# Spread indirect transfers, second norms as row scales, one ranking for all tokens, and a chunk's rows weighed on VectorE

## The reference

```python
# layer 0: state-space branch, two sequences of 1024, chunks of Q=128, 64 heads of 8
Yd     = einsum('bcijh,bcjhp->bcihp', CB * Lmat * dtc, xs_c)       # within a chunk
wdec   = exp(cum[:, :, -1:, :] - cum) * dtc
states = einsum('bcqh,bcqhn,bcqhp->bchpn', wdec, Bc, xs_c)         # rows weighed by decay
yn     = yz * rsqrt(mean(yz * yz) + EPS) * norm_w
# layer 0 and layer 3: mixture of 8 experts, 2 of them per token (plus a shared one in layer 0)
top_w, top_ids = top_k(probs, 2);  out = sum over the 2 experts of w * expert(x)
# layer 2: xn2 = ln(xn) * ln_scale + ln_bias, prev = shift(xn2)
kx = xn2 * mix_k + prev * (1 - mix_k)      # the same with mix_v and mix_r
# then a scan over 256 steps with a running maximum, and a quantised gated ffn
# layer 3: x1 = ln(xn, ln1_g, ln1_b); xln = ln(x1, tm_g, tm_b); then a shift, a mix, products
```

## Time and profile before

| | |
|---|---|
| median of 3 runs | 1617.82 us (1613.74 to 1619.62) |
| the profiled execution | 1622.43 us, span 1620.6 us |
| mean granted clock of PE | 0.895 |
| layer 0 | about 0 to 639 us |
| layer 1 | to about 918 us |
| layer 2 | to about 1169 us |
| layer 3 | to the end |

### The profile page before, as it was taken

One profiled execution on the slowest core, in us unless ns is written; L12 is line 12 of the kernel. 1 busy time (PEld: TensorE's weight loads), 2 busy tenths in 40 slices (PEclk: granted clock), 3 DMA queues, 4 the chain that ended last, 5 costly groups with the idle time before them and its releaser, 6 DMA issues. The chain is left out here.

```text
span 1620.6 us, 21650 instructions
## 1 busy us (share of the span) xinstructions
PE 1323.1 (82%) x7251; PEld 818.1 (50%) x7251; DVE 936.6 (58%) x1888; ACT 534.5 (33%) x885; POOL 412.4 (25%) x380
## 2 busy tenths in 40 slices
PE   5765988897898556999999897898556599988997
PEld 3433645555564334657666544454343364644464
DVE  6767565664646874213103489898676445567434
ACT  1454356536535530222222231333112123233311
POOL 3278224313528641200400110000015300000035
PEclk9877999998989676999999898999856698999999
DMA  9232113212213222100000230000001100111113
GB/s 357 67 90 80 43 35 107 63 40 79 83 29 107 75 66 74 39 0 1 0 0 0 105 129 1 0 1 1 1 3 65 59 20 27 33 39 56 53 49 117
DMA packets 72082, 88.86 MB, mean 55 GB/s; under 512 B 19174, under 2 KB 55334, under 8 KB 71337
## 3 DMA queue, kind: packets, MB, share of 16 engines
q1 hardware_dynamic: 65836, 70.78, 14.1%
q0 software_dynamic: 6144, 16.79, 3.3%
HBM read 61.14 MB, written 26.38 MB: 54 GB/s over the span
## 5 line engine op out<-in xcount | busy, mean ns | idle before, releaser
L398 PE MATMUL l_banks<-l_xnT,all_region_a 128*128 128x512 f32 x288 | 129.0, 601 | 0.0
L1877 PE MATMUL l_banks<-l_xnT,mid_region_c 128*128 128x512 f32 (+1 forms) x192 | 96.3, 654 | 17.5 <-DVE l_xnT L2060 17.5
L2720 POOL TENSOR_TENSOR l_rstd<-l_moments,all_neg_half 128x4 f32<-128x4 f32 x20 | 20.6, 1030 | 337.5 <-DVE l_moments L2760 337.4
L914 POOL TENSOR_TENSOR all_region_b<-all_region_b,l_lc 128x512 f32<-128x512 f32 x64 | 87.8, 1393 | 36.5 <-DMA all_region_b<-l_lc_rows 36.1
L928 POOL TENSOR_TENSOR l_rw<-l_xdt,l_decay 128x512 f32<-128x512 f32 x64 | 71.8, 1152 | 63.9 <-DVE l_xdt L1171 63.9
L1191 DVE TENSOR_TENSOR all_region_b<-all_region_b,l_cbd 128x512 f32<-128x512 f32 x64 | 77.6, 1213 | 16.3 <-ACT all_region_b L746 12.2
L398 PEld LDWEIGHTS l_banks<-l_xnT,all_region_a 128*128 128x128 f32 x288 | 54.5, 193 | 61.5 <-issue 60.3
L398 PE MATMUL l_banks<-all_region_b,l_xp 128*32 128x32 f32 x2048 | 32.3, 208 | 62.9 <-DVE all_region_b L1191 62.8
L746 ACT ACTIVATE all_region_b<-all_region_b 128x512 f32<-128x512 f32 x64 | 69.0, 1079 | 14.6 <-PE l_banks L398 10.4
L1877 PEld LDWEIGHTS l_banks<-l_xnT,mid_region_c 128*128 128x128 f32 (+1 forms) x192 | 37.7, 202 | 68.3 <-issue 49.6
L398 PE MATMUL l_banks<-all_region_a,all_xa 128*128 x234 | 68.8, 418 | 1.3 <-DVEq L1040 0.4
(11 more groups left out here) (442 smaller groups left out, 2883.6 us busy)
## 6 DMA issues: line engine op xcount, KB each, us to landing
all_region_b<-l_lc_rows SPq DMA_DIRECT2D x256, 64.0 KB, 2.1
all_xa<-slots_in SPq DMA_DIRECT2D x39, 128.0 KB, 2.1
slots_out<-all_xa SPq DMA_DIRECT2D x39, 128.0 KB, 2.0
mid_vector_rows<-slots_in SPq DMA_DIRECT2D x39, 128.0 KB, 2.1
slots_out<-all_region_a SPq DMA_DIRECT2D x39, 128.0 KB, 1.7
slots_in<-l_xp SPq DMA_DIRECT2D x4, 1024.0 KB, 12.7
all_region_a<-l_gate_up SPq DMA_DIRECT2D x1, 4096.0 KB, 14.4
all_x<-x SPq DMA_DIRECT2D x4, 512.0 KB, 5.6
```

The source lines that it names most:

```text
L398: return nc.tensor.matmul(out, lhsT, rhs, start=start, stop=stop, **kw)
L914: nc.gpsimd.tensor_tensor(bc[:, k, :, :], bc[:, k, :, :], spread(lc[:, c, heads], 1, BLK), ALU.subtract).then_inc(dd_ready.sem, 1)
L1877: return nc.tensor.matmul(out, lhsT, rhs, start=start, stop=stop)
L2720: nc.gpsimd.tensor_tensor(rstd[:, :], moments[:, :, 1], mem.neg_half[:, 0:GT], ALU.pow).then_inc(rstd_ready.sem, 1)
```

## The change

It has eight parts.

A. `steps_at`: the expert tile steps of layer 0 stand after the 32 pieces from (0,3) to (2,2), with every third doubled (10 of them), where they stood after 36 pieces from (0,3) to (2,3), with six doubled. Chunk (0,3) has 5 instead of 4, group 1 has 21 instead of 20, chunks 0 to 2 of group 2 have 16 instead of 14, and chunk (2,3) has none instead of 4.

B. `weigh` is DVE's, behind `take_cb` of the same chunk; `take_xs` needs no wait for the weighed rows any longer.

C. Scatters of layer 0: 8 issues instead of 16 ahead of the first differences, 4 behind them, the rest between the differences of the chunks; the last 6 stand behind `differences(0,3)`.

D. Fetches: 12 issues (t = 2 to 7) move from group 3 into chunk (2,3), and the other 20 all stand ahead of group 3's chunk loop, 8 of them behind `differences(3,0)`.

E. At the end of layer 0 the last `out_stats` stands ahead of `quantise(1)` on DVE.

F. Layer 2: the second norm is one scale per row, worked out on POOL from the first norm's variance, and ACT applies it (`norm_again`, four activations). DVE measures xn no more. The mix is one subtraction of 128x1024 per group and 6 instructions of 128x512.

G. Layer 3: all groups' second norm scale is worked out at once on POOL (128x16), `nl` is four scalings and one addition of 128x1024, ACT copies both turned halves into one of two buffers, and the ranking is done once for all 16 tiles (`rank`).

H. `PLAN` and `beside` are reordered for it: `nl`, `nm` of groups 0 and 1 stand behind `dispatch`.

The diff, cut (the removed `weigh` is POOL's, the added one DVE's; the added `norm_again` is ACT's, in layer 2):

```diff
-    places = [(g, c, k) for g in range(GROUPS - 1) for c in range(NCH) for k in range(PIECES) if (g, c) >= (0, 3)]
-    places = sorted(places + [places[4 * i + 6] for i in range(STEPS - len(places))])
+    places = [(g, c, k) for g in range(GROUPS - 1) for c in range(NCH) for k in range(PIECES)
+              if (0, 3) <= (g, c) < (GROUPS - 2, NCH - 1)]
+    places = sorted(places + [places[3 * i + 2] for i in range(STEPS - len(places))])
...
-        def weigh(g, c):
-            pool.wait_ge(xs_ready.sem, xs_ready.done(g, c))
...
-                last = nc.gpsimd.tensor_tensor(rw[:, i, :].rearrange("p (h e) -> p h e", e=HEAD_P), x3,
-                                               spread(decay[:, i, c, :], 2, HEAD_P), ALU.mult)
...
+            if t == GT // 2:
                 for i in range(2):
                     pool.wait_ge(moe.oe_out[i], 16 * ((MOE_TILES - i + 1) // 2))
...
-        late = {0: ((8, 9), (10, 11)), 1: ((12, 13), (14, 15))}
+        late = {0: ((6,), (7, 8)), 1: ((9, 10), (11, 12)), 2: ((13, 14, 15), ())}
...
             if g == GROUPS - 1:
-                for t in range(2 * GT):
+                for t in (*range(GT // 2), *range(2 * GT, 3 * GT)):
                     fetch(t)
...
+                elif g == GROUPS - 2:
+                    for t in range(GT // 2, 2 * GT):
+                        fetch(t)
...
-                if g == GROUPS - 1:
-                    for t in ((12, 13), (14,), (15,), ())[c]:
-                        fetch(t)
...
+        def weigh(g, c):
...
+            for i in range(4):
+                last = nc.vector.tensor_tensor(by_head(rw[:, i, :]), by_head(xdt[:, :]),
+                                               spread(decay[:, i, c, :], 2, HEAD_P), ALU.mult)
+            last.then_inc(rw_ready.sem, 1)
...
                 if c + 1 < NCH:
                     take_cb(g, c + 1)
+                    weigh(g, c + 1)
...
+        out_stats(GROUPS - 1, NCH - 1)
         quantise(1)
-        out_stats(GROUPS - 1, NCH - 1)
...
+        def norm_again(g):
+            act.wait_ge(xn_ready.sem, xn_ready.done(g))
+            act.wait_ge(rstd2_ready.sem, rstd2_ready.done(g))
+            for t in range(GT):
+                last = nc.scalar.activation(x2[:, t, :], xn[:, t, :], ACT.Copy, scale=rstd2[:, g * GT + t:g * GT + t + 1])
+            last.then_inc(x2_ready.sem, 1)
...
+            nc.gpsimd.tensor_tensor(rstd2[:, tiles], moments[:, tiles, 1], rstd[:, tiles], ALU.mult)
+            pool.drain()
+            nc.gpsimd.tensor_tensor(rstd2[:, tiles], rstd2[:, tiles], rstd[:, tiles], ALU.mult)
+            pool.drain()
+            nc.gpsimd.tensor_scalar(rstd2[:, tiles], rstd2[:, tiles], 1e-5, None, ALU.add)
+            pool.drain()
+            nc.gpsimd.tensor_tensor(rstd2[:, tiles], rstd2[:, tiles], mem.neg_half[:, tiles], ALU.pow).then_inc(
+                rstd2_ready.sem, 1)
...
+            if i == 0:
+                nc.vector.tensor_tensor(step[:, :, :], x2T[:, :, 1:], x2T[:, :, 0:GROUP], ALU.subtract)
...
-    PLAN = [("nx", 0), ("nx", 1), ("consts", 0), ("turn_x", 0), ("nx", 2), ("route", 0), ("turn_x", 1), ("bias", 0),
-            ("nx", 3), ("route", 1), ("turn_x", 2), ("ml", 0), ("nl", 0), ("route", 2), ("turn_x", 3), ("nm", 0),
-            ("route", 3), ("dispatch", 0), ("scatter", 0), ("turn_l", 0), ("ml", 1), ("nl", 1), ("mix", 0),
-            ("scatter", 1), ("nm", 1), ("turn_l", 1), ("scatter", 2), ("scatter", 3), ("weights", 0), ("mix", 1),
+    PLAN = [("mx", 0), ("mx", 1), ("nx", 0), ("turn_x", 0), ("mx", 2), ("nx", 1), ("turn_x", 1), ("route", 0),
+            ("mx", 3), ("consts", 0), ("pl", 0), ("nx", 2), ("turn_x", 2), ("route", 1), ("nx", 3), ("turn_x", 3), ("route", 2),
+            ("route", 3), ("rank", 0), ("dispatch", 0), ("scatter", 0), ("nl", 0), ("bias", 0), ("nm", 0),
+            ("scatter", 1), ("turn_l", 0), ("nl", 1), ("mix", 0), ("scatter", 2), ("nm", 1), ("scatter", 3),
+            ("turn_l", 1), ("weights", 0), ("mix", 1), ("scatter", 4), ("scatter", 5), ("time_row", 0), ("scale", 0),
```

More of the change, by code:

```diff
@@ L970, in _ @@
             if g == GROUPS - 1:
-                for t in range(2 * GT, 3 * GT):
+                for t in range(3 * GT, 4 * GT):
                     fetch(t)
-            weigh(g, 0)
+            if g == 0:
+                for t in range(GT, GT + 2):
+                    scatter(t)
             for c in range(NCH):
@@ L1808, in layer2 @@
     rstd = sb("rstd", [P, TILES])
-    moments2 = sb("moments2", [P, GT, 2])
-    rstd2 = sb("rstd2", [P, GT])
+    above = sb("above", [P, TILES])
+    rstd2 = sb("rstd2", [P, TILES])
     xn = sb("xn", [P, GT, DIM])
@@ L1813, in layer2 @@
     x2T = sb("x2T", [P, DK, 1 + GROUP])
-    keep = sb("keep", [P, 3, DK])
     part = sb("part", [P, DK, GROUP])
     x2 = part[:, :, :].rearrange("p a n -> p (a n)").rearrange("p (t d) -> p t d", t=GT)
-    q = part
+    q = step = part
     mixed = sb("mixed", [P, 3, DK, GROUP])
@@ L1963, in _ @@
                              ACT.Exp).then_inc(decay_exp, 1)
+        norm_again(0)
         for g in range(groups):
@@ L1991, in _ @@
                 nc.scalar.activation(buf[:, :, :], buf[:, :, :], ACT.Exp).then_inc(exp_ready.sem, 1)
+            if g + 1 < groups:
+                norm_again(g + 1)
     @block.gpsimd
@@ L2027, in statistics @@
             tiles = slice(n * GT, (n + 1) * GT)
-            nc.vector.tensor_scalar(moments[:, tiles, 1], moments[:, tiles, 1], 1e-5, None, ALU.add).then_inc(
+            nc.vector.tensor_scalar(above[:, tiles], moments[:, tiles, 1], 1e-5, None, ALU.add).then_inc(
                 moments_ready.sem, 1)
@@ L2187, in _ @@
         take_xnT(0)
-        norm_again(0)
         for g in range(groups):
@@ L2214, in _ @@
             sums(g)
-            if g + 1 < groups:
-                norm_again(g + 1)
             if g == 0:
@@ L2278, in layer3 @@
     rc = sb("rc", [P, GT, DIM])
-    lmax = sb("lmax", [P, GT])
-    pairs = GT * N_EXP * N_EXP
-    gt, eq = [junk[:, i * pairs:(i + 1) * pairs].rearrange("p (t e f) -> p t e f", e=N_EXP, f=N_EXP) for i in range(2)]
+    lmax = sb("lmax", [P, TILES])
+    moments_x = sb("moments_x", [P, TILES, 2])
+    rstd_x = sb("rstd_x", [P, TILES])
+    above = sb("above", [P, TILES])
+    rstd_l = sb("rstd_l", [P, TILES])
+    pairs = TILES * N_EXP * N_EXP
+    gt, eq = [b[:, 0:pairs].rearrange("p (t e f) -> p t e f", e=N_EXP, f=N_EXP)
+              for b in (rc[:, :, :].rearrange("p t d -> p (t d)"), xcT[:, :, :].rearrange("p k n -> p (k n)"))]
+    rows_T = [xnT, mixT]
     vm = sb("vm", [P, HALVES, DK])
@@ L2789, in route @@
+        def norm_x(g):
+            dve.wait_ge(rstd_ready.sem, rstd_ready.done(0, norm_at["nx", g]))
+            for t in range(g * GT, (g + 1) * GT):
+                last = nc.vector.tensor_scalar(xn[:, t, :], x[:, t, :], moments_x[:, t, 0:1], rstd_x[:, t:t + 1],
+                                               ALU.subtract, ALU.mult)
+            last.then_inc(normed_ready.sem, 1)
         def route(g):
-            tiles = slice(g * GT, (g + 1) * GT)
-            l4 = lg[:, tiles, :]
             jobs.wait_filled(dve, 0, ("route", g))
-            last = nc.vector.tensor_tensor(l4, jobs.bank(("route", g))[:, 0:GT * N_EXP].rearrange(
-                "p (t e) -> p t e", e=N_EXP), spread(row("router_bias"), 1, GT), ALU.add)
+            last = nc.vector.tensor_tensor(lg[:, g * GT:(g + 1) * GT, :], jobs.bank(("route", g))[
+                :, 0:GT * N_EXP].rearrange("p (t e) -> p t e", e=N_EXP), spread(row("router_bias"), 1, GT), ALU.add)
```

186 lines of the change are left out of this document (91 added, 95 removed).

## The result

The changed kernel takes 1579.24 us (median of 4, 1578.46 to 1580.08) against 1616.32 us (median of 4, 1613.74 to 1619.62). The ratio is 0.977, with a 95% interval of 0.9749 to 0.979: 2.3% faster. The forecast was 1584 us with a range of 1562 to 1607.

What follows compares the result with a forecast made beforehand. PE was taken to bound the whole, waiting some 300 us. The terms -13 + 0 - 12 - 10 + 1 = -34 us gave 1588.4 on the profiled scale, 4.6 us above the median, so 1584 us; range 1562 to 1607.

Steps and rivals of the forecast that it cites:

- the late scatters: Layer 0, group 0: six scatters behind the last differences, 8.4 us, taken as hidden, with up to +5 as the end.
- The step by which chunk (2,3) loses four tile steps: Layer 0, chunk (2,3): without its four tile steps it falls from 22.7 to 16 us, -6.7.
- The three added tile steps: Layer 0, groups 1 and 2: three more tile steps where PE is the bound, 2.4 us each, +7.2.
- The two terms of the weighing there: Groups 1 and 2: `near` no longer slowed beside the weighing, -6; weighing on DVE delaying PE, +5.5.
- The cover: Group 3: DVE's 12.8 us wait for PE's output product covers 2.7 us of added weighing per chunk; without it +8.
- the half that the prediction took of the stalls of the additions: Group 3: additions slowed beside four POOL differences, 9 us in two chunks; half of it was taken as gained, -5.
- the -3 for the fetches: Group 3: four fetches and the weighing no longer stand between `gate` and POOL's next differences, -3 us.
- The product: Layer 2, DVE: 3.24 us beside POOL's addition, 1.4 at most without; 1.9 us gained in each of three transitions.
- The slower one: Layer 0: DVE's weighing delays the tile step and next `near` in 15 places, +41; 1639 us, chance 0.06.
- The lock that changes sides: Layer 0, groups 0 and 3: DVE's weighings each wait for one POOL difference, +29 in six chunks; 1613 us, chance 0.12.
- The clock of the last group: Layer 0: PE's clock may rise with fewer waits, argued for everything giving its upper end, -61; 1557 us, chance 0.10.
- The scatters of layer 3: Layer 3: each power waits for DVE's norms, so scatters come later, +8 instead of +1; 1591 us, chance 0.08.

Runs made afterwards that it cites:

- The addition moved alone: Kernel before, with POOL's layer 2 addition of xn to x issued ahead of the second power, nothing else of part F: ratio 0.9937 (0.9915 to 0.996).

## Why the prediction was right

**Group 0: the sum right, the terms no finer than the traces allow.** The `take_y` instructions moved by -11.1, -12.2, -15.9 and -13.3 us: -11 for the start, about nothing in chunk 1, -4 in chunk 2, and +2.6 in chunk (0,3), against -11, 0, -4 and +2.4. That the late scatters would be hidden held: chunk (0,3) takes 20.3 us with C and with C undone. What the sum did not say is that the -11 has two owners, each of which is enough: B alone gives 108.70, and the other parts without B 107.53. That the terms agree to half a microsecond is in part luck. The old layer 0 has its first `take_y` at 115.2 to 120.6 in four traces, and chunk (0,1) took 18.1 us in the changed kernel and 22.3 in a trace with the same code up to there.

**Groups 1 and 2: +3.1 instead of 0, and part A was wrong.** The step by which chunk (2,3) loses four tile steps and with them 6.7 us failed: the chunk is 17.3 us long without tile steps, and 17.8 or 18.2 with them in the runs of B, of F and of G and H alone. The 22.7 us of the earlier trace rows were not its only length: of four traces of the same layer 0, two show 18.2 and two 22.7. Against 18.2, A gave back 0.9 us, and the change lengthened this stretch by some 8 us, not 3.1. The three added tile steps were priced at 7.2 us; up to the `take_y` of (2,2) the changed kernel takes 8.7 us more than B alone, 2.9 us for each. All four kernels with A undone and the fetches moved back had lower ratios than the changed one, 0.9701 to 0.9762 against 0.977. The two terms of the weighing there, -6 and +5.5, came to nothing together, as they should: 283.8 us with B alone, 283.8 and 284.0 without.

**Group 3: -16.5 instead of -12, the mechanism right, the size low.** The cover held: DVE's wait for PE's output product fell by 2.5 us in each of two chunks, for 2.7 us of weighing, and came back when the weighing went back to POOL. What was too small is the half that the prediction took of the stalls of the additions, -5, and the -3 for the fetches: both additions that had stood still for 5.4 us came down to at most 1.5, not one of them. Up to its last `take_y` the group got 13.7 us shorter, 7.6 with B alone, where both stalls are still there, and 6.1 more with the other parts, which take the fetches out of its loop. The earlier `out_stats`, to which the prediction gave no term, gave 2.8 us (from the last `take_y` to layer 1, 17.4 us with B alone and 14.6 after).

**Layer 2: -12.6 instead of -10, the mechanism right, the size low.** Up to the first product nothing changed, and from there to the last one the three transitions gave 3.8, 5.2 and 4.8 us, where 3.3 was forecast for each; behind the last product 1.3 us were lost. The product gave 5.8 us, as in the sum (three times 1.9). The addition moved alone gave 8.8 us in the three transitions, which is 3 more than the product. The other 5 are `norm_again`, counted at 4.2, and the measurement and half of the mix, counted at nothing; no run takes these apart.

**Layer 3: -2.2 instead of +1 to the first tile.** The first scatter came 6.1 us sooner, not 3.3. Ranking all tiles once took 7.1 us, close to the 7.7 of the sum; the other 2 us are in the new order of the front and were not resolved. The powers among the scatters cost 3.9 us. The prediction has 4 and 0.6 for them, and the 4.3 of the table comes of its rounding to +1.

**The rule against it.** By the Trainium skill, "SBUF — State Buffer", section "Who interferes with whom", the lock is held for one whole instruction, so that a blocked engine waits for one instruction of the other. In the changed kernel a `near` waited through four differences (5.61 us). With a drain between them none took more than 1.75 us, its own 0.69 and about one difference. So the rule agrees with the trace of spaced instructions, and a row without gaps acted as one long lock.

**The rivals.** The slower one had the weighing on the path everywhere, 2.7 us in 15 places. It did not come: groups 1 and 2 were as long with B alone as without, and in group 3 DVE's wait covered it. The lock that changes sides did not come: the weighings took 685 ns in the median, and one of 64 took 4.34 us. The clock of the last group did not rise. The scatters of layer 3 did not come late.

**How close it was.** In the medians the forecast was 5 us off. In the traces it was 9: -34 against -42.7, of which the long chunk (2,3) of the profiled execution before is 4.5 us. Part of the closeness is that errors cancelled: A cost some 8 us in groups 1 and 2, and group 3, layer 2 and layer 3 gave about 10 more than forecast. The half-widths of the five parts, taken as independent, make 12 us and not the 15 that the prediction states; the range does not hang on it.

What stays open: in two kernels with 16 scatters ahead of the first differences (C undone) the first `take_y` was 10 us later, and with the same scatters and B alone it was not. The two are from chip 5 and B alone is from chip 0, so the chip is a rival that no run excludes. Neither this nor the condition under which PE waits for "issue" beside the fetches was settled. A run of the changed kernel on chips 5 and 8 would be the first step.

## What to carry to other kernels

Look for instructions of one engine that are longer beside another engine's than alone, and count how many of the other's stand in one row without a gap: moving work off the blocking engine can pay although the other engine, which is closer to the bound, gets all of it. When two edits remove instructions from the same blocking row, price them together, since a stall goes only once. Before shifting work out of a stage, check that the stage is bound by that work: here four steps cost at most 1 us together in (2,3), and 2.9 us each elsewhere. When variants are run in several sets, put the changed kernel itself into each: a stretch of the same code was 11 us longer on two chips, and only traces of other variants showed that it was not the edit. One trace of a stretch is one sample; the 22.7 us on which a term rested was 18.2 in half of the traces.

## What the runs showed of the hardware

PE could stand still while POOL issued indirect transfers one behind the other, waiting for nothing that the profile shows; that it ran short of instructions is a guess. In six traces PE's waits put down to "issue" are 7 to 11 us in one such row of 12 or 16 transfers, in pieces of up to 2.7 us, and end about as the row ends; all six are from chips 5 and 8. In the trace of the changed kernel and in that with B undone (chip 0) the same row of 12 passes without them. A row of POOL instructions without gaps held a DVE instruction for its whole length (5.61 us for four, 9.72 for eight); a drain of 0.16 us between them limited this to 1.75 us.
